# Head loop of a graph-attention kernel: reciprocal row sums spread through DRAM, and the leaky activation shared between ScalarE and GpSimd

## The reference, cut to what matters

```python
def gat_layer(x, graph, W, b):
    h = x @ W
    s = jnp.einsum('bnd,bmd->bnm', h, h) * graph
    s = jnp.where(s == 0.0, NEG_INF, s)
    a = jax.nn.softmax(s, axis=2)
    return jnp.einsum('bnm,bmd->bnd', a, h) + b
heads = jax.vmap(lambda W, b: gat_layer(flow_x, graph, W, b))(Wh, bh)
x = jax.nn.leaky_relu(cat, negative_slope=0.01)     # cat: the heads side by side
out = gat_layer(x, graph, W_out, b_out)
```

## Time and profile before

| | us |
|---|---|
| time, median of 3 runs | 3390.31 (3386.8 to 3392.65) |
| the profiled execution: its run | 3389.07 |
| its span, first to last instruction | 3387.3 |
| one item of the head loop in steady state | 55.62 |
| DVE, PE, ACT, GpSimd busy in such an item | 54.78, 54.65, 42.32, 2.36 |

### The profile page before, as it was taken

One profiled execution on the slowest core, in us unless ns is written; L12 is line 12 of the kernel. 1 busy time (PEld: TensorE's weight loads), 2 busy tenths in 40 slices (PEclk: granted clock), 3 DMA queues, 4 the chain that ended last, 5 costly groups with the idle time before them and its releaser, 6 DMA issues. The chain is left out here.

```text
span 3387.3 us, 48344 instructions
## 1 busy us (share of the span) xinstructions
PE 3089.4 (91%) x15547; PEld 1885.1 (56%) x15547; DVE 2982.4 (88%) x3851; ACT 2300.4 (68%) x3525; POOL 830.0 (25%) x580
## 2 busy tenths in 40 slices
PE   7998899999999999999999999799598888888857
PEld 3676566666666666666666666599554333333323
DVE  3578999999999999999999999688756999999944
ACT  0122677777777777777777777677346999999831
POOL 0123000000000000000000000000114999999921
PEclk9999999999999999999999999899799999999978
DMA  4000000000000000000000000000000000000001
GB/s 97 0 1 1 1 1 0 0 0 0 0 0 0 0 0 0 0 0 0 0 0 0 0 0 0 1 1 0 9 0 1 1 1 1 1 1 1 1 2 25
DMA packets 30364, 12.16 MB, mean 4 GB/s; under 512 B 27984, under 2 KB 29264, under 8 KB 30288
## 3 DMA queue, kind: packets, MB, share of 16 engines
q1 hardware_dynamic: 25056, 10.04, 1.3%
q10 hardware_dynamic: 5232, 1.12, 0.2%
HBM read 9.06 MB, written 2.10 MB: 3 GB/s over the span
## 5 line engine op out<-in xcount | busy, mean ns | idle before, releaser
L660 ACT ACTIVATE hid_work<-hid_work,hid_nmax 128x1024 f32<-128x1024 f32 x512 | 589.5, 1151 | 305.5 <-DVE hid_nmax L644 305.5
L632 DVE TENSOR_TENSOR hid_work<-hid_score_ps,A 128x1024 f32<-128x1024 f32 x512 | 618.3, 1208 | 30.0 <-PE hid_score_ps L593 29.9
L644 DVE CUSTOM_DVE_ANT_0 hid_work<-hid_masks,hid_work 128x1024 f32<-128x1024 f32 x512 | 620.6, 1212 | 0.2 <-DVE hid_masks L652 0.2
L1690 POOL TENSOR_TENSOR el<-el,node_edge 128x1024 f32<-128x1024 f32 x256 | 610.5, 2385 | 17.8 <-DVE el L1672 11.5
L671 ACT COPY hid_probsT<-hid_turn_ps 128x512 f32<-128x512 f32 x1024 | 542.2, 580 | 101.9 <-PE hid_turn_ps L607 101.9
L607 PEld LDWEIGHTS hid_turn_ps<-ident,hid_work 128*128 128x128 f32 x4096 | 458.4, 141 | 249.3 <-issue 206.0
L607 PE MATMUL hid_turn_ps<-ident,hid_work 128*128 128x128 f32 x4096 | 544.9, 276 | 4.9 <-ACT hid_probsT L671 3.9
L818 PE MATMUL hid_mix_ps<-hid_probsT,x_now 128*64 128x512 f32 x2048 | 497.2, 606 | 33.4 <-DVE hid_Zn L892 30.5
L592 PE MATMUL hid_score_ps<-hid_SX,hid_Y 128*128 (+1 forms) x1024 | 476.9, 466 | 2.6 <-DVE hid_SX L993 2.6
L593 PE MATMUL hid_score_ps<-hid_SX,hid_Yl 128*128 (+1 forms) x1024 | 405.5, 396 | 0.0
L1643 PE MATMUL spread<-hT_parts,pick 128*128 128x512 f32 x1024 | 309.2, 425 | 65.9 <-DVE u_buf L1666 61.6
(11 more groups left out here) (280 smaller groups left out, 4080.2 us busy)
## 6 DMA issues: line engine op xcount, KB each, us to landing
A<-in_adj_dram SPq DMA_DIRECT2D x4, 1024.0 KB, 9.8
X<-in_x_dram SPq DMA_DIRECT2D x8, 256.0 KB, 8.8
out_dram<-X SPq DMA_DIRECT2D x8, 256.0 KB, 3.4
wa<-in_L_gnn_weight_dram ACTq DMA_DIRECT2D x2, 256.0 KB, 15.2
wb<-in_L_gnn_weight_dram ACTq DMA_DIRECT2D x2, 256.0 KB, 13.6
wh<-in_L_gnn_Wh_dram SPq DMA_DIRECT2D x2, 256.0 KB, 5.5
incid<-in_L_gnn_H_dram SPq DMA_DIRECT2D x2, 256.0 KB, 3.5
wo<-in_L_gnn_W_out_dram SPq DMA_DIRECT2D x1, 256.0 KB, 6.1
```

The source lines that it names most:

```text
L632: nc.vector.tensor_tensor(work[:, kk % 4, :], score_ps[kk % 2][:], A[:, kk % NT, :], ALU.mult).then_inc(s["weighted"], 1)
L644: nc.vector.tensor_tensor_reduce(work[:, kk % 4, :], masks[:, kk % 2, :], work[:, kk % 4, :], -1.0, 3.0e38, ALU.add, ALU.min, nmax[:, kk % ...
L660: nc.scalar.activation(work[:, kk % 4, :], work[:, kk % 4, :], ACT.Exp, bias=nmax[:, kk % 4:kk % 4 + 1], scale=-1.0, accum_out=rowsum[:, k ...
L1690: nc.gpsimd.tensor_tensor(el[:, q % ELS, :], el[:, q % ELS, :], coefT[:, q // C, :], ALU.mult).then_inc(s_weighted, 1)
```

## The change

It has two parts, both in the head loop.

The four transposes `R` and ACT's copy to `rbc` are gone. Instead SP stores the 128x4 reciprocals as 128 rows of 16 bytes into a DRAM tensor, waits for that, and loads the 2 KB back into every partition of `rbc`. Column `4q + a` of `rbc` now belongs to row `q` of tile `a`, so `vec_norm` reads it with a step of four elements (16 bytes); before, the step was one.

The leaky activation is made as `0.01 y + relu(99 * 0.01 y)`: ACT writes `sloped = 0.01 y` (from PSUM, bias scaled beforehand by GpSimd), then, after the copies of the same step, `leaky = relu(99 sloped)`, from SBUF to SBUF. GpSimd adds the two (`pool_leaky`, both inputs in SBUF). DVE's instruction is gone. `act_relu` and `pool_leaky` run once each in steps 2, 6, 10, 14.

```diff
-            EARLY = {0: ("R", 8), 2: ("W", 14), 4: ("R", 8), 6: ("W", 14), 8: ("R", 8), 10: ("W", 14), 12: ("R", 8),
-                     14: ("W", 14)}
+            EARLY = {2: ("W", 14), 6: ("W", 14), 10: ("W", 14), 14: ("W", 14)}
...
-                if EARLY[k][0] == "R":
-                    pe.wait_ge(s["inverted"], g + 1)
-                    pe.nop(nofuse=True)
-                    for a in range(GROUP):
-                        slot = u * NT + half * GROUP + a
-                        done = nc.tensor.transpose(misc_ps[:, a * P:(a + 1) * P],
-                                                   at.rinv[:, slot:slot + 1].to_broadcast([P, P]), ident[:])
...
-                    nc.scalar.copy(rbc[:], misc_ps[:]).then_inc(misc_read, 1)
-                else:
-                    nc.scalar.activation(leaky[:, u, half, :], misc_ps[:], ACT.Identity,
-                                         bias=bh_now[:]).then_inc(misc_read, 1)
+                if k == 6 and not first:
+                    act.wait_ge(leaky_made, 4 * i - 3)
+                    act.nop(nofuse=True)
+                nc.scalar.activation(sloped[:, half, :], misc_ps[:], ACT.Identity, bias=bh_now[:],
+                                     scale=SLOPE).then_inc(misc_read, 1)
+
+            def act_relu(act, i, k, first, last):
+
+                if not present(k, False, first, last):
+                    return
+                g, u, half, _ = group_of(i, k, EARLY[k][1])
+                act.wait_ge(misc_read, use(i, k, False, first, last) + 1)
+                act.nop(nofuse=True)
+                nc.scalar.activation(leaky[:, u, half, :], sloped[:, half, :], ACT.Relu,
+                                     scale=1.0 / SLOPE - 1.0).then_inc(relu_made, 1)
...
-                vec.wait_ge(misc_read, use(i, k, False, first, last) + 1)
-                nc.vector.scalar_tensor_tensor(out=part, in0=part, scalar=0.01, in1=part, op0=ALU.mult,
-                                               op1=ALU.max).then_inc(leaky_made, 1)
+                pool.wait_ge(relu_made, 1 if first else 4 * i - 2 + k // 4)
+                pool.nop(nofuse=True)
+                nc.gpsimd.tensor_tensor(part, part, sloped[:, half, :], ALU.add).then_inc(leaky_made, 1)
...
+                if not first:
+                    vec.wait_ge(r_stored, 64 * i + 16 * ((k - 6) // GROUP) - 32)
+                    vec.nop(nofuse=True)
                 nc.vector.reciprocal(at.rinv[:, slots], at.rowsum[:, slots]).then_inc(s["inverted"], 1)
...
-                vec.wait_ge(misc_read, use(i, k - 2, False, first, last) + 1)
+                vec.wait_ge(r_loaded, 64 * i + 16 * ((k - 10) // GROUP + 1))
                 vec.nop(nofuse=True)
-                nc.vector.tensor_tensor(Zn[:, half, :], mix_ps[:], rbc[:], ALU.mult).then_inc(s["normed"], 1)
+                nc.vector.tensor_tensor(Zn[:, half, :].rearrange("p (a q) -> p a q", a=GROUP),
+                                        mix_ps[:].rearrange("p (a q) -> p a q", a=GROUP),
+                                        rbc[:].rearrange("p (q a) -> p a q", a=GROUP), ALU.mult).then_inc(s["normed"], 1)
...
+            def sp_body(sp, i, first=False):
+
+                for d in range(4):
+                    sp.wait_ge(s["inverted"], 4 * i + d + 1)
+                    sp.nop(nofuse=True)
+                    sp.dma_start(r_rows[d], at.rinv[:, d * GROUP:(d + 1) * GROUP]).then_inc(r_stored, 16)
+                    if not first or d >= 1:
+                        sp.wait_ge(s["normed"], 4 * i + d)
+                        sp.nop(nofuse=True)
+                    sp.wait_ge(r_stored, 64 * i + 16 * (d + 1))
+                    sp.nop(nofuse=True)
+                    sp.dma_start(rbc[:], r_rows[d].rearrange("q a -> (q a)").unsqueeze(0).to_broadcast([P, HALF])
+                                 ).then_inc(r_loaded, 16)
+                    sp.wait_ge(r_loaded, 64 * i + 16 * (d + 1))
+                    sp.nop(nofuse=True)
```

More of the change, by code:

```diff
@@ L545, in adjacency_stack_kernel @@
         MASKED = -1.0e16
+        SLOPE = 0.01
         BODY = 2 * NT
@@ L765, in pe_early @@
                 g, u, half, ib = group_of(i, k, EARLY[k][1])
-                if EARLY[k][0] == "R":
-                    pe.wait_ge(s["inverted"], g + 1)
-                    pe.nop(nofuse=True)
-                    for a in range(GROUP):
-                        slot = u * NT + half * GROUP + a
-                        done = nc.tensor.transpose(misc_ps[:, a * P:(a + 1) * P],
-                                                   at.rinv[:, slot:slot + 1].to_broadcast([P, P]), ident[:])
-                else:
[L774 to L778, removed]
+                if u == 0 and half == 0:
+                    pe.wait_ge(staged_w, ib + 1)
+                pe.wait_ge(s["normed"], g + 1)
+                pe.nop(nofuse=True)
+                done = nc.tensor.matmul(misc_ps[:], wh_now[:], Zn[:, half, :], start=True, stop=True)
                 done.then_inc(misc_made, 1)
@@ L863, in vec_late, with pool_leaky @@
                     nc.vector.tensor_tensor(acc, acc, misc_ps[:].unsqueeze(1), ALU.add).then_inc(misc_read, 1)
-            def vec_leaky(vec, i, k, first, last):
-                if not present(k, False, first, last) or EARLY[k][0] != "W":
-                    return
+            def pool_leaky(pool, i, k, first=False, last=False):
                 _, u, half, _ = group_of(i, k, EARLY[k][1])
                 part = leaky[:, u, half, :]
-                vec.wait_ge(misc_read, use(i, k, False, first, last) + 1)
-                nc.vector.scalar_tensor_tensor(out=part, in0=part, scalar=0.01, in1=part, op0=ALU.mult,
-                                               op1=ALU.max).then_inc(leaky_made, 1)
+                pool.wait_ge(relu_made, 1 if first else 4 * i - 2 + k // 4)
+                pool.nop(nofuse=True)
+                nc.gpsimd.tensor_tensor(part, part, sloped[:, half, :], ALU.add).then_inc(leaky_made, 1)
             def vec_invert(vec, i, k, first, last):
@@ L906, in act_step @@
                 at.act_copy(act, i, k, first, last)
+                act_relu(act, i, k, first, last)
             def vec_step(vec, i, k, first=False, last=False):
@@ L910, in vec_step @@
                 vec_norm(vec, i, k, first, last)
-                if k:
-                    vec_leaky(vec, i, k - 1, first, last)
                 at.vec_shift(vec, i, k, first, last)
@@ L939, in pool_body @@
                 if not first:
+                    pool_leaky(pool, i, 2)
                     pool.wait_ge(s["mixed"], 4 * i)
@@ L946, in pool_body @@
                 if not first:
+                    pool_leaky(pool, i, 6)
+                    pool_leaky(pool, i, 10)
                     pool.wait_ge(misc_read, use(i, 10, False, first, False) + 1)
@@ L952, in pool_body @@
                 stage_x(pool, bass.ds((i + 1) // HEADS % J, 1), 0)
+                pool_leaky(pool, i, 14, first)
                 if not first:
@@ L962, in adjacency_stack_kernel, with _ @@
             block = scope.enter_context(nc.Block())
+            @block.sync
+            def _(sp):
+                sp_body(sp, 0, first=True)
+                with sp.Fori(1, ITEMS) as i:
+                    sp_body(sp, i)
             @block.gpsimd
@@ L967, in _ @@
                 stage_x(pool, bass.ds(0, 1), 0)
+                nc.gpsimd.tensor_scalar(bh[:], bh[:], SLOPE, None, ALU.mult).then_inc(cleared, 1)
+                pool.wait_ge(cleared, 1)
                 nc.gpsimd.memset(h2T[:], 0.0).then_inc(cleared, 1)
@@ L971, in _ @@
                     pool_body(pool, i)
+                for k in (2, 6, 10):
+                    pool_leaky(pool, ITEMS, k, last=True)
             @block.scalar
@@ L1003, in _ @@
                     x_lo(b)
-                vec.wait_ge(cleared, 1)
+                vec.wait_ge(cleared, 2)
                 bodies(vec, vec_step, ITEMS)
```

13 lines of the change are left out of this document (6 added, 7 removed).

## The result

The changed kernel takes 3499.96 us (median of four runs, 3496.16 to 3500.36) against 3388.56 us (3384.19 to 3392.65) for the kernel before on the same chip. The ratio is 1.0326, with a 95% interval of 1.0309 to 1.0344: the change costs 3.3%. The profiled execution has a span of 3494.4 us, 107.1 more than the span of before.

The account below looks back on a forecast made before the run. The prediction took DVE and PE, holding each other in the head loop, as the bound. From 3389.1 us: -76.8 (leaky) -26 (idle) +131 (lock) +46 (step) +3 (tail) = 3466 us, range 3395 to 3515.

Parts of the forecast that it names:

- The bound: Head loop: DVE (54.78 us of 55.62 an item) and PE (54.65) hold each other; DVE's 0.84 us idle goes.
- The lock and its place: Steps 2, 6, 10, 14: GpSimd's sum, requested during the shift, delays DVE's zero step 1.05 us; +131 us in all.
- the rival that lived on the shortness of the margin: GpSimd's sum waits until the zero step is over, costing DVE nothing: 3337 us, 3371 with `Zn` +0.36; chance 0.13.
- The step: `Zn` reading `rbc` with a step of 16 bytes: +0.36 us each on DVE, +46 us in all.
- The transfers: Store and load of reciprocals through DRAM: 5.5 to 10.9 us, nearest 5.5, in 10.9 of room; put at nothing.
- The rival of late transfers: Store and load exceed their 10.9 us and hold `Zn`; at 11.5 us +77 us; chance 0.04.
- The mis-sized term: DVE's stream in one item of the head loop: 52.38 + 4.20 + 1.44 = 58.0 us.
- The tail: Three GpSimd sums after the head loop stand on the path where DVE took 0.6 us: +3 us.

Follow-up runs that it names:

- The gated sum: The changed kernel with each GpSimd sum held until the zero step of the same step is over: 3373.8 us, ratio 0.9950 to the kernel before.
- the plain step: The changed kernel with reciprocals stored transposed in 4-byte pieces, so that `Zn` reads `rbc` with a step of one: 3763.56 us, ratio 1.1101.
- the spread alone: The changed kernel with the leaky activation given back to DVE, keeping the transfers through DRAM: 3421.62 us, ratio 1.0091 to the kernel before.
- the activation alone: The changed kernel with the reciprocals spread by PE again, keeping the leaky activation on ACT and GpSimd: 3437.99 us, ratio 1.0140.

## Why the prediction was right, point by point

- **The bound.** Said: the two engines hold each other, and what is put back on DVE decides. DVE is busy 1700.00 us of 1700, as said, and the 0.84 us of idle time are gone. The median of 3499.96 us lies 34 us above the 3466 forecast, inside the range of 3395 to 3515, in its upper half: a rise of 76 us was forecast, and 111 came.
- **The lock and its place.** Said: the request falls into the shift, GpSimd gets on at the shift's end, and zero waits in steps 2, 6, 10 and 14. All of that stands in the timeline. The margin does not: 0.33 us before the end of the shift was said, 0.87 was found (1000.96 to 1001.83). The forecast had placed the shift behind a `Zn` of the old length, though it put 0.36 us on `Zn` elsewhere; the longer `Zn` moves the shift's end from 2.88 to 3.25 us behind the weigh. The sum in turn comes 2.38 us behind it and not 2.55, as ACT's relu took 0.64 instead of 0.69 and GpSimd started 0.14 behind it instead of 0.25. So the rival that lived on the shortness of the margin had less behind it than was said. The size was 1.08 for 1.05: +4 us. The gated sum then priced this rival: it was put at 3371 with `Zn` at +0.36, and 3373.8 was measured. The page "SBUF — State Buffer" of the Trainium skill ("Who interferes with whom"), which lists `tensor_scalar` among the instructions that can take the lock, is borne out by 1.76 us for 0.68.
- **The step.** Said: +0.36 by L421; measured +0.37 between starts (0.97 for 0.60). The rule on the same page of the Trainium skill ("SBUF: two separate sides", a step of up to 4 fp32 free) does not hold for this instruction: 1056 ns with a step of 4 fp32 (median), 678 and 691 with a step of one.
- **The transfers.** Said: 5.5 us, in 10.9 us of room, so nothing. Measured 1.4 + 4.1 us, and no wait in the loop. The room did not grow with the longer items, though that was said: in the item shown it is 9.7 to 10.7 us from the reciprocal's end to `Zn`, and that was still enough. The rival of late transfers did not come about in this layout; the kernel with the plain step showed its price: rows some 4 us beyond the room, and an item of 67.2 us for 59.0.
- **The mis-sized term.** Most of the 34 us, 25 of them, is one thing that the sum did not have: GpSimd's own copies of `x_now`. They were in the kernel before and cost nothing there, so their line was read as unchanged. But the trace of before has one start at 1030.29 beside a zero step of 1029.51 to 1030.11, 0.18 us behind its end, released by a burst of PE (kernel before, GpSimd; then DVE):

```profile
1030.29 0.62 POOL L934 COPY x_now<-X 128x512 f32 x1 [22.33 <-PE hid_mix_ps L818]
```

```profile
1029.51 0.68 DVE L652 TENSOR_SCALAR hid_masks<-hid_work 128x1024 f32<-128x1024 f32 x1
```

Counted from the start of the zero step, the copy came 0.78 us behind it before, and it comes 0.11 us ahead of it in the kernel after (1009.22 for 1009.33). With the spread alone it stands between the two (kernel with the spread alone, GpSimd; then DVE):

```profile
1016.26 0.80 POOL L927 COPY x_now<-X 128x512 f32 x1 [10.29 <-PE hid_mix_ps L812]
```

```profile
1015.90 0.68 DVE L653 TENSOR_SCALAR hid_masks<-hid_work 128x1024 f32<-128x1024 f32 x1
```

There it comes 0.36 us behind the start, within the zero step: the copy waits (0.80 us for 0.61), and DVE loses nothing. The change gives PE room against DVE, and PE releases the copies earlier; with the activation alone, where PE keeps its `R`, they come 1.0 us behind the start. The price is 2 x 0.40 an item, and 26 us came back when the copies were held. The term that was too small is "DVE's stream becomes 52.38 + 4.20 + 1.44 = 58.0": the stream was 58.98, of which 0.80 are the copies, 0.12 the lock and 0.04 `Zn`. The prediction had moved the waits between PE and DVE and had not asked which third engine is released by PE and meets DVE at a new moment.
- **The tail.** Said +3; the difference of the spans less 31 items leaves 2.

## What to carry to other kernels

Work that is moved to GpSimd within SBUF was free in this kernel where it ran beside VectorE instructions that read PSUM, and cost DVE nearly its own length in front of one that works within SBUF. Look up where its request will fall in VectorE's order, and if it falls onto a pair of SBUF instructions, a wait on GpSimd's side is cheaper than the collision (here 126 us). A layout that saves a transfer's small pieces was paid by the reader on VectorE, so both must be priced: 0.37 us for each product here against a load that goes out some 8.5 us later. When the balance between two engines changes, go through everything that a third engine does at the release of either one, even what the change does not touch.

## What the runs showed of the hardware beyond the forecast

- A GpSimd copy with one SBUF input (128x512) holds up VectorE's `tensor_scalar` like a sum: 1.08 us for 0.68. Who waits goes by who comes first: a copy that comes 0.11 us ahead of the zero step holds it up, one that comes 0.36 us into it waits itself.
- A zero step lost 1.08 us to a sum of 512 columns and 0.55 to one of 256.
- A store of 128x4 values from SBUF to DRAM took 1.4 us in 16-byte pieces; in 4-byte pieces the load that waits for it went out 9.96 us later.
- GpSimd's held-up time shows as busy time: 2.07 us for a sum that takes 1.27 when nothing holds it up. A busy GpSimd is not a working one.
- In the kernel with the plain step, PE's granted clock is 0.50 in a stretch behind 4.03 us of idle time, and a burst of eight products takes 3.68 us instead of 1.94.
